# Gated cross-attention and expert layer on one core: records of 132 words, ScalarE forms the residual, another order of the half steps

## What is computed

```python
x = x + tanh(g_xattn[0]) * xattn(layernorm(x), ctx, ctx, W_qkv, b_qkv, W_out, b_out)
x = x + tanh(g_ffn[0]) * moe(layernorm(x), Wg, W1, b1, W2, b2)

# xattn, per batch and head (SCALE = 8 ** -0.5)
attn = softmax(q @ k.T * SCALE);  out = (attn @ v) merged over heads @ W_out + b_out
# moe (C = 4096 / 8 = 512)
gates = softmax(tokens @ Wg); idx = argmax(gates)        # first-come places, C per expert
hidden = relu(rows_of_expert @ W1[e] + b1[e]);  y = hidden @ W2[e] + b2[e]
out[token] = gate * y                                    # tokens beyond C get 0
```

## Time and profile before

| | us |
|---|---|
| median of 3 runs | 298.25 (296.54 to 298.52) |
| the profiled execution's own time | 298.6 |
| its span, from first to last instruction | 296.5 |
| PE busy, share of span | 244.5, 82% |
| DVE | 196.6, 66% |
| POOL | 182.3, 61% |
| ScalarE | 155.6, 52% |
| mean granted TensorE clock | 0.937 |
| DMA moved | 39.27 MB |

### The profile page before, as it was taken

How to read it: one execution, slowest core, us unless ns; L and a number is a source line. 1 busy time by engine, 2 the same in 40 slices (tenths; PEclk the granted TensorE clock), 3 DMA queues, 4 the chain that set the end, 5 groups by cost and what they waited for, 6 DMA issues and landing times.

```text
span 296.5 us, 8184 instructions
## 1 busy us (share of the span) xinstructions
PE 244.5 (82%) x2907; PEld 163.5 (55%) x2907; DVE 196.6 (66%) x663; ACT 155.6 (52%) x375; POOL 182.3 (61%) x246
## 2 busy tenths in 40 slices
PE   1748758788979989999899989995869999999950
PEld 1325525465755755765656666663324677777740
DVE  4676717647978999989897999965302545555440
ACT  5553727567778787787887756681202322222100
POOL 6625916911982998897897968448720056555781
PEclk9998959969999999999999999999595999999995
DMA  4652771990482652661733541138352256554310
GB/s 120 184 162 73 214 217 32 237 293 19 113 235 57 174 158 71 195 182 46 213 110 90 152 126 57 58 102 174 138 144 66 71 170 188 173 180 132 103 55 16
DMA packets 50920, 39.27 MB, mean 132 GB/s; under 512 B 9698, under 2 KB 47223, under 8 KB 50880
## 3 DMA queue, kind: packets, MB, share of 16 engines
q1 hardware_dynamic: 47168, 28.67, 35.9%
q0 software_dynamic: 3712, 10.07, 10.4%
HBM read 13.72 MB, written 12.65 MB: 89 GB/s over the span
## 4 chain that ended last, share of the span: by engine, by line
PE 39%; DVE 13%; DMA 13%; SPq 10%; issue 9%; ACT 8%; POOL 4%; POOLq 0%; ACTq 0%; DVEq 0%
PE X L634 9%; DMA qp<-mrow 8%; DVE negm L833 6%; SPq L347 6%; PE TS L618 5%; PE M L546 3%; ACT prob L703 3%; PE O L513 3%; PE TS L497 3%; PE O L618 3%; PE M L618 2%; PE S L482 2%; PE X L441 2%; SPq L358 2%; POOL rec_dram L1224 2%
## 5 line engine op out<-in xcount | busy, mean ns | idle before, releaser
L703 ACT ACTIVATE prob<-TS 128x512 f32<-128x512 f32 x128 | 72.0, 589 | 40.1 <-PE TS L497 39.2
L833 DVE TENSOR_REDUCE negm<-S 128x4 f32<-128x512 f32 x128 | 81.6, 679 | 8.5 <-PE S L482 7.9
L513 PE MATMUL O<-prob,vals 128*32 128x128 f32 x1024 | 42.1, 283 | 0.8 <-ACT oraw L712 0.8
L1313 POOL DMA_INDIRECT out_dram<-fin,tok x32 | 31.5, 986 | 14.2 <-issue 12.2
L1224 POOL DMA_INDIRECT rec_dram<-rec,slot x32 | 32.2, 1005 | 8.0 <-issue 5.5
L497 PE MATMUL TS<-qp,kp 64*128 64x128 bf16 x512 | 28.1, 221 | 9.7 <-DMA qp<-mrow 9.6
L482 PE MATMUL S<-kp,qp 62*128 62x128 bf16 x512 | 31.3, 222 | 2.3 <-DVE negm L833 2.0
L513 PEld LDWEIGHTS O<-prob,vals 128*32 128x32 f32 x1024 | 24.6, 110 | 13.9 <-ACT prob L703 7.0
L267 POOL TENSOR_TENSOR rest_k<-full_k,parts_k 128x512 f32<-128x512 f32 x7 | 8.0, 1149 | 39.3 <-ACT parts_k L674 39.3
L804 ACT ACTIVATE qp<-TS,b_act 128x512 f32<-128x512 f32 x16 | 11.0, 687 | 39.9 <-PE TS L618 39.9
L634 PE MATMUL X<-w2s,qp 128*128 128x128 f32 x240 | 28.2, 275 | 0.9 <-issue 0.9
(11 more groups left out here) (170 smaller groups left out, 486.8 us busy)
## 6 DMA issues: line engine op xcount, KB each, us to landing
kp<-parts_k SPq DMA_DIRECT2D x48, 128.0 KB, 2.5
qp<-parts_q SPq DMA_DIRECT2D x48, 128.0 KB, 4.1
rec_dram<-zeros POOLq DMA_DIRECT2D x8, 516.0 KB, 6.2
xr<-rec_dram SPq DMA_DIRECT2D x8, 260.0 KB, 3.9
x_sb<-in_x_dram SPq DMA_DIRECT2D x8, 256.0 KB, 3.6
c_sb<-in_ctx_dram SPq DMA_DIRECT2D x8, 256.0 KB, 3.5
out_dram<-rec SPq DMA_DIRECT2D x8, 256.0 KB, 3.3
w1s<-in_L_ffn_W_dram SPq DMA_DIRECT2D x8, 256.0 KB, 4.1
```

The costliest lines, as they stand in the source:

```text
L513: mm = nc.tensor.matmul(o_out[i * HV:(i + 1) * HV, u * L:(u + 1) * L], vals[G % 2][:, k, h, :], prob[n % 2][:, h * L:(h + 1) * L], start=( ...
L703: nc.scalar.activation(prob[n % 2][:, first:first + 4 * L], TS[:, a, :], ACT.Exp).then_inc(a_exp, 1)
L833: V.tensor_reduce(negm[n % 2][:, first:first + 4], S[:, a, :].rearrange("p (h k) -> p h k", k=L), AX.X, ALU.max, negate=True).then_inc(v_r ...
L1313: G_.indirect_dma_start(out_rows, bass.IndirectOffsetOnAxis(tok[p][:, t:t + 1], 0), fin[p][:, t, :], None, bounds_check=T - 1, oob_is_err= ...
```

## The change

- **Records** have 132 words: gate, token code, mean, deviation, then the 128 normalised values. Gate and code take the place of two of the logits in `rec`, the moments are aggregated right behind them, and the scatter sends from there. POOL gets one more multiplication per group, `deviation` (deviation = (var + eps) * (var + eps) ** -0.5). The zero writes and the scatters shrink with the record; `load_xr` goes, `load_xe` takes whole records into three buffers instead of two.
- **ScalarE** forms x1 again as normalised * deviation + mean (`rows_again`: four activations per expert), and DVE's `residual2` adds b2 * gate to that.
- **Heads** are numbered (h a) instead of (a h), so that one multiplication does the normalising instead of two.
- **Order of a step, PE**: scores u=0, shifted u=0, values u=0, maxima transpose, oT of c-5, group work, scores u=1, shifted u=1, values u=1, back, at, group work. Bank X0 now holds oT and at, M the maxima and back; xT and q move to X1.
- **Order of a step, ScalarE**: oraw of batch c-3 after the second exponentials, onT of c-5 after the first.
- **Order of a step, DVE**: top u=0, lower part, top u=1, normalise, residual, moments, group work.
- **SyncE** stores x1 of a group in step j = 1 instead of j = 0. POOL's scatters in a step wait for the lower part instead of the residual.

```diff
-REC = 2 * P + 2
+REC = P + 4
@@ x_tasks
-            bank0 = [("at", c - 5), second]
-            bank1 = [first, third]
-            bank2 = [("m", c - 1), ("back", c - 4), ("oT", c - 4)]
+            bank0 = [second] if c < 0 else [("oT", c - 5), ("at", c - 5)]
+            bank1 = [first, third] if c < 0 else [first, third, second]
+            bank2 = [("m", c - 1), ("back", c - 4)]
@@ SyncE, step
-                loads, stores = j == 0 and is_group(g + 2), j == 0 and is_group(g - 2)
+                loads, stores = j == 0 and is_group(g + 2), j == 1 and is_group(g - 2)
@@ SyncE, experts
-                sp.dma_start(xe[e % 2][:], rec_v[e][:, :, 0:D]).then_inc(xe_in[e % 2], 16)
-            def load_xr(e):
-                sp.dma_start(xr[e % 2][:], rec_v[e][:, :, D:REC]).then_inc(xr_in[e % 2], 16)
+                sp.dma_start(xe[e % 3][:], rec_v[e]).then_inc(xe_in[e % 3], 16)
...
@@ PE, step
                 if is_batch(c - 2):
                     shifted(c - 2, 0)
+                if is_batch(c - 3):
+                    values(c - 3, 0, 0)
+                    values(c - 3, 0, 1)
                 if is_batch(c - 1):
...
                     nc.tensor.transpose(m_out, negm[(c - 1) % 2][:], ident).then_inc(p_m, 1)
+                if is_batch(c - 5):
+                    bank_free(pe, "oT", c - 5)
+                    pe.wait_ge(v_on, c - 4)
+                    nc.tensor.transpose(oT_out, on[(c - 5) % 2][:], ident).then_inc(p_oT, 1)
...
+                if is_batch(c - 5):
+                    bank_free(pe, "at", c - 5)
+                    pe.wait_ge(a_oT, c - 4)
+                    nc.tensor.matmul(X[:, 0, 0:DE], onT[(c - 5) % 2][:], wout_g[:], start=True, stop=True).then_inc(p_at, 1)
@@ ScalarE, experts
+            def rows_again(e):
+                act.wait_ge(xe_in[e % 3], 16 * (e // 3) + 16)
+                if e >= 3:
+                    act.wait_ge(fin_out[e % 3], 64 * (e // 3))
+                for t in range(ET):
+                    mm = nc.scalar.activation(fin[e % 3][:, t, :], xe[e % 3][:, t, 4:], ACT.Identity,
+                                              bias=xe[e % 3][:, t, 2:3], scale=xe[e % 3][:, t, 3:4])
+                mm.then_inc(a_res, 1)
...
                 nc.scalar.activation(xeT[p][:], S[:, p, :], ACT.Copy).then_inc(a_eT, 1)
+                if e >= 1:
+                    rows_again(e - 1)
+                if e == E - 1:
+                    rows_again(e)
@@ DVE, normalise
-                for a in range(2):
-                    mm = V.tensor_tensor(on[n % 2][:, a * HALF:(a + 1) * HALF].rearrange("p (h d) -> p h d", d=HD),
...
+                V.tensor_tensor(on[n % 2][:].rearrange("p (h d) -> p h d", d=HD), o[:, :, 0:HD],
+                                rl[:].unsqueeze(2).broadcast_to([P, HEADS, HD]), ALU.mult).then_inc(v_on, 1)
@@ DVE, step
-                if is_batch(c - 5):
-                    residual(c - 5)
-                if is_batch(c - 4):
-                    normalise(c - 4, g - 2 if j == 0 and is_group(g - 2) else None)
...
                 if is_batch(c):
                     top(c, 1)
+                if is_batch(c - 4):
+                    normalise(c - 4)
+                if is_batch(c - 5):
+                    residual(c - 5)
@@ DVE, residual2
-                p = e % 2
...
+                dve.wait_ge(a_res, e + 1)
                 for t in range(ET):
                     mm = V.scalar_tensor_tensor(fin[p][:, t, :], b2_all[:, e, :], gate2[p][:, t:t + 1],
-                                                xr[p][:, t, 0:D], ALU.mult, ALU.add)
+                                                fin[p][:, t, :], ALU.mult, ALU.add)
@@ POOL
+            def deviation(G):
+                pool.wait_ge(g_rs2, G + 1)
+                G_.tensor_tensor(rec[G % 3][:, :, DEV], rs2[:, 0, :], rs2[:, 1, :], ALU.mult).then_inc(g_dev, 1)
...
-                G_.indirect_dma_start(rec_dram, bass.IndirectOffsetOnAxis(slot[p][:, k:k + 1], 0), rec[p][:, k, 0:REC], None,
+                G_.indirect_dma_start(rec_dram, bass.IndirectOffsetOnAxis(slot[p][:, k:k + 1], 0), rec[p][:, k, GATE:], None,
...
                 if j < 3 and is_group(g - 3) and g - 3 < NG - 2:
-                    pool.wait_ge(v_x1, min(c - 4, B))
+                    pool.wait_ge(v_m, min(c, B))
                     scatter(g - 3, j + 1)
```

More of the change, by code:

```diff
@@ L42, in flamingo_kernel @@
     DE = D + E
+    GATE, CODE, MEAN, DEV, NORMED = DE - 2, DE - 1, DE, DE + 1, DE + 2
     HEADS = 16
@@ L136, in flamingo_kernel @@
         st2 = sb("st2", [P, GB, 6])
-        mv2 = sb("mv2", [P, GB, 2])
         rs2 = sb("rs2", [P, 2, GB])
         nm2 = sb("nm2", [P, GB])
-        rec = [sb(f"rec{i}", [P, GB, D + DE]) for i in range(3)]
+        rec = [sb(f"rec{i}", [P, GB, NORMED + D]) for i in range(3)]
         lmax = sb("lmax", [P, GB])
@@ L161, in flamingo_kernel @@
         b1_dve = [sb(f"b1_dve{i}", [P, 1, FC]) for i in range(2)]
-        xe = [sb(f"xe{i}", [P, ET, D]) for i in range(2)]
-        xr = [sb(f"xr{i}", [P, ET, REC - D]) for i in range(2)]
+        xe = [sb(f"xe{i}", [P, ET, REC]) for i in range(3)]
         xeT = [sb(f"xeT{i}", [P, CAP]) for i in range(2)]
@@ L166, in flamingo_kernel @@
                for i in range(2)]
-        gate2 = [sb(f"gate2_{i}", [P, ET]) for i in range(2)]
-        tok = [sb(f"tok{i}", [P, ET], U32) for i in range(2)]
-        fin = [sb(f"fin{i}", [P, ET, D]) for i in range(2)]
+        gate2 = [sb(f"gate2_{i}", [P, ET]) for i in range(3)]
+        tok = [sb(f"tok{i}", [P, ET], U32) for i in range(3)]
+        fin = [sb(f"fin{i}", [P, ET, D]) for i in range(3)]
         s_cst, s_wqkv, s_bias, s_late = sem("s_cst"), sem("s_wqkv"), sem("s_bias"), sem("s_late")
@@ L412, in _ @@
                 load_w2(e)
-                sp.wait_ge(v_res, e - 1)
-                load_xr(e)
             for p in range(3):
                 sp.wait_ge(x1_out[p], 16 * len(range(p, NG, 3)))
-            for p in range(2):
-                sp.wait_ge(fin_out[p], 16 * ET * (E // 2))
+            for p in range(3):
+                sp.wait_ge(fin_out[p], 16 * ET * len(range(p, E, 3)))
         @block.tensor
@@ L532, in step @@
                     nc.tensor.transpose(m_out, negm[(c - 1) % 2][:], ident).then_inc(p_m, 1)
+                if is_batch(c - 5):
+                    bank_free(pe, "oT", c - 5)
+                    pe.wait_ge(v_on, c - 4)
+                    nc.tensor.transpose(oT_out, on[(c - 5) % 2][:], ident).then_inc(p_oT, 1)
                 for t in at_q[0]:
                     group_task(t[0], t[1])
-                if is_batch(c - 5):
-                    bank_free(pe, "at", c - 5)
-                    pe.wait_ge(a_oT, c - 4)
-                    nc.tensor.matmul(X[:, 0, 0:DE], onT[(c - 5) % 2][:], wout_g[:], start=True, stop=True).then_inc(p_at, 1)
+                if is_batch(c):
+                    scores(c, 1)
+                if is_batch(c - 2):
+                    shifted(c - 2, 1)
                 if is_batch(c - 3):
-                    values(c - 3, 0, 0)
-                    values(c - 3, 0, 1)
+                    values(c - 3, 1, 0)
+                    values(c - 3, 1, 1)
                 if is_batch(c - 4):
@@ L665, in proj @@
                 bias = bq_s[:, 0:1] if side == 0 else bqk[:, 1:2]
-                nc.scalar.activation(full[side][:], X[:, side, :], ACT.Identity, bias=bias,
+                nc.scalar.activation(full[side][:], X[:, 1, :] if side else q_bank(H), ACT.Identity, bias=bias,
                                      scale=(SCALE, 1.0)[side]).then_inc((a_qf, a_kf)[side], 1)
@@ L722, in step @@
                     exps(c - 2, 0, 1)
+                if is_batch(c - 5):
+                    n = c - 5
+                    act.wait_ge(p_oT, n + 1)
+                    if n >= 2:
+                        act.wait_ge(p_at, n - 1)
+                    nc.scalar.activation(onT[n % 2][:], oT_out, ACT.Copy).then_inc(a_oT, 1)
                 if j == (2 if g + 2 else 1) and is_group(g + 2):
@@ L1043, in step @@
                     top(c, 1)
+                if is_batch(c - 4):
+                    normalise(c - 4)
+                if is_batch(c - 5):
+                    residual(c - 5)
+                if j == 0 and is_group(g - 2) and g - 2 < NG - 1:
+                    moments2_ready(g - 2)
+                    moments2(g - 2)
+                if c == B + 4:
+                    route2(NG - 1)
+                    place2(NG - 1)
                 if j == 0 and is_group(g):
@@ L1154, in _ @@
             finish(E - 2, 0)
+            residual2(E - 1)
             finish(E - 2, 1)
             relus(E - 1)
-            residual2(E - 1)
             finish(E - 1, 0)
@@ L1168, in fence, with root @@
                 return G_.tensor_tensor(fence_p[:], pool_c[:, 0, 0:1], pool_c[:, 0, 0:1], ALU.add).then_inc(g_fence, 1)
-            def root(H, mv, rs, ready, e):
+            def root(H, var, rs, ready, e):
                 pool.wait_ge(ready, H + 1)
```

(5 more changed lines are left out.)

140 lines of the change are left out of this document (59 added, 81 removed).

## The result

The changed kernel takes 295.38 us (median of 20 runs, 293.02 to 302.56), the kernel before 298.38 beside it (20 runs). The ratio is 0.989, 95% interval 0.986 to 0.993: 1.1% faster, 3.2 us.

The account below looks back on a forecast made before the run. DMA traffic was taken to bound the first steps, with neither PE nor DVE free in steady attention. Early -5.5, steady -1.5 and bridge +1.9 sum to -5.1 from 298.6, so 293.5 us; 8 in 10 range 289 to 299.5.

Parts of the forecast that it names:

- likeliest case: Whole kernel: early steps and bridge as costed, steady steps within 3 us, 290.5 to 297 us; chance 0.55.
- steady term: Steady attention: -0.4 us per group over about 4 full groups, -1.5 us in all; bounds -6 and +6.
- early term: First steps: shorter zero writes free 6.0 us of path, later maxima DMAs cost 0.5; -5.5 us, bounds -2 and -8.
- bridge: Between attention and experts: the late row sum starts POOL about 1.5 us later; +1.9 us, bounds +0.4 and +3.
- sum by the fit: Whole kernel: by the fixed-cost DMA rule seven shorter zero writes give 4.1 us, and the sum would be 295.4.
- Scatters and loads: POOL's scatters and the load behind the last: width does not set issue time; 0, scatter bounds -0.3 to +0.2 us.
- ScalarE's residual: Experts: 1.9 us more ScalarE work per expert, covered by PE's outputs; 0, bounds 0 to +1 us.
- First expert: Experts: no gain was forecast, blocks were to keep the same length.
- A: First steps: zero writes do not hold the early landings, packs also fill the queues; early -1.5, 297.5 us; chance 0.2.
- B: Whole kernel: the order wins PE's idle back; early -7, steady -4.5, bridge +0.5, 287.6 us; chance 0.15.
- C: Steady attention: DVE loses its cover, maxima DMA lands late, 0.7 us in 3 steps of 7 groups; 306.9 us; chance 0.1.

Follow-up runs that it names:

- a_zero516: The changed kernel with each zero write as long as before (516 KB), records still 132 words: 303.58 us, 1.019 of the kernel before.
- a_store_j3: The changed kernel with the store of a group's rows in the fourth step of a group instead of the second: 296.13 us, 0.990 of before.
- a_maxima_first: The changed kernel with the maxima transpose ahead of the first half's values again on PE: 302.97 us, 0.978 of before.
- b_records2: The kernel b_records run again on another chip: 300.54 us, 0.967 of before.
- b_zero_gated: The kernel before with its full-size zero writes issued four at a time, POOL first waiting for the maxima rows of steps 3 and 7: 0.996 of before.
- r_dummies11: b_records with eleven dummy matmul pairs instead of eight ahead of the first expert: 300.89 us, 0.974 of before.
- r_best: b_records with ten dummy matmul pairs and its zero writes four at a time behind the lower parts of steps 3 and 7: 298.69 us, 0.969 of before.
- a_at_early: The changed kernel with, from the last scores on, PE's row sum ahead of the second values and DVE's residual ahead of normalise: 301.89 us, 0.970 of before.
- b_records: The kernel before with 132-word records, ScalarE's residual and three buffers, but its own order, banks, store and head numbering: 290.39 us, 0.976 of before.
- b_order: The kernel before with the new order, banks, head numbering and store in the second step, but records of 258 words: 313.89 us, 1.020 of before.

## Why the prediction was right, and where it was off

The direction and the likeliest case held, and 295.4 lies inside the case's own range of 290.5 to 297; 60% of the forecast gain came. It lies there in part by luck: the steady term was wrong by 3.7 us, and the early term, the bridge and an unforeseen gain in the first expert together made up 2.2 of them. Term by term:

**Early, -5.5.** Right in mechanism and size: -6.4 in the profiles at step 8, where a_zero516 stands 7.3 us behind after; in time it loses 1.0188 less 0.9893, 3.0% or 9 us (7.5 us against a_store_j3 on its own chip), so the extra bytes cost a little later on too. The size is read with care, as the same writes gave 3.2 us at step 8 in a_store_j3. My working scaled engine time with bytes. In 30:42 the share fell to 0.62 instead of 0.51 of what it was, in 53:67 to 0.30, since the writes there were over sooner. The Trainium skill (DMA: Bandwidth & Descriptors, the fixed-cost fit under "Anatomy of one DMA") gives, as an estimate, 4.1 us for the writes. The runs show 6.4 to 9 us. The fit is of one DMA; what transfers in full queues do to each other is seen here in 5.7 against 3.7 us of landing in 30:42, where the fit has 0.6 us between the two sizes. That the sum by the fit was 295.4, the time measured, is chance: both its early and its steady term were off.

**Steady, -1.5.** This is the step that failed, in its sign: +2.2 us from step 8 to 32. Two of the gains I listed came (`onT` 2.3 and the load's 1.3 us gone). The third did not: DVE's wait for the transposed output, 0.3 us a group to be saved, grew from 1.6 to 3.7 us in four. Of the losses I had DVE's idle before the reductions at 0.9 per group; it rose from 1.0 to 2.8 us in four, half of that. Missing was the other direction: PE's scores wait for DVE's reductions of the scores before, 4.2 us in 13 pieces. And I gave the later maxima rows 0.1 to 0.3 per group, where PE's wait for them rose by 0.7 (2.3 to 5.0 in four). I had followed that loop from DVE's side and counted the transpose's own shift; the table above shows the term that counts, PE's work between the transpose and the shifted scores, which the new order cuts from 4.6 to 3.57 us. Both lines stood in the trace of before: the transpose of the earlier trace rows and the wait of 0.71 on the next step's rows. New PE waits of 6.9 us less 3.6 gone are +3.3 in the window, of the size of the +2.2 to step 32. But the waits' own length is not what counts most: 1.3 of the 2.2 us go in the one step with the low clock behind the first wait, where two matmuls of 512 columns take 1.52 us (82.91) and 1.02 a group later at the same line. I had no term for that. Against the records alone on a like chip the order costs 3.8 to 4.4 us in steps 8 to 25. What stays open is the share of each piece in the time: no run took the wait for the maxima rows away whole, and those that moved it (a_store_j3, a_maxima_first) left waits between scores and reductions.

**Bridge, +1.9.** Right: +1.6 in the order's two kernels, 0.0 in the records alone, and POOL's idle grew by 1.75 us (4.74 to 6.49) where I had 1.5. Scatters and loads: 0 as said; a scatter takes 1003 ns for 132 words and 1005 for 258, and the last lands after 2.18 us instead of 2.30.

**ScalarE's residual, 0.** Right. Its group in after (line, engine, what, count, busy us, mean ns, idle before it):

```profile
L797 ACT ACTIVATE fin<-xe 128x128 f32<-128x128 f32 x32 | 13.0, 481 | 0.0
```

It is 13.0 us more of ScalarE, and from the third expert on an output block still takes PE 3.57 us, as in the earlier trace rows; nothing on PE waits for it.

**First expert, 0.** Unforeseen, -1.2 us. In both traces the clock is at 0.50 for a stretch that begins behind the last dummy: from 216.4 to 223.2 us in after, from 221.7 to 228.5 in before. After's turn starts later behind the dummies (4.8 us, 2.0 before), so only 4.6 us of this stretch fall on the expert's work, 6.8 before. These 2.2 us less at half the clock are worth 1.1 us, an estimate from the traces; the block is 6.7 us against 7.9. The other traces fit: 4.8 to 4.9 us where no low stretch touches the block (b_records2, b_zero_gated, r_dummies11, r_best), 6.5 and 6.6 with 3.4 us of one (a_at_early, b_records). What makes the clock fall in some and not in others I did not test.

**The rivals.** A fell with a_zero516. B fell: the order wins nothing back. C's mechanism is there, at a third of its size or less (2.8 us of DVE's waits in four groups, 1.0 of them before too, against 2.1 a group); but its condition, a later landing, was not what did it: the DMA took 1.98 to 2.53 us on after's chain in these steps.

## What to carry to other kernels

Where a tiny DMA is on the path and the queues are full, look for the bulk transfer that shares them and cut its bytes; moving it in time won at most 1% here, halving it 3%. Before an order is called neutral, measure for each round trip between engines how long the answer takes and how much work the asker has meanwhile (5.2 against 3.57 us here), and look at the waits in both directions, and at the granted clock behind each wait: one wait of 1.75 us cost 1.3 us with the low clock behind it, two of its size without it 0.1 and 0.9. A change with two halves deserves a run of each half: the good one (2.4%) carried a bad one (2.0% by itself, 1.4% by difference).

## What the runs showed of the hardware

- The same 4 KB transfer of maxima rows, where the chain runs through it, takes 1.98 to 2.53 us in after's steady steps, 3.5 and 3.9 in its early ones, 4.1 to 6.2 beside the long zero writes (before, a_zero516; 3.3 to 5.7 in b_order) and 8.45 behind a burst of four.
- Four writes of 516 KB issued within 3.2 us hold a 128 KB pack on the chain for 10.61 us.
- POOL's issue of a scatter takes 1003 ns with rows of 132 words and 1005 with 258.
- Of 15 waits of PE for the maxima rows of 1.5 to 2.6 us (steps 8 to 25, six kernels in the new order), 7 have a stretch at 0.50 of the clock on their heels. The five kernels that have one or two of them give back 2.2 to 5.0 us in these steps, the one without 0.4.
- In six of the eight profiles from the slower chips (all but a_at_early and a_maxima_first) one DVE instruction that computes places, on 128x4 elements and mostly 0.2 us long elsewhere, takes 1.7 to 2.1 us at 163 to 176 us, and the granted clock falls to 0.50 within 4 us. What holds it up no run shows.
- Chips differ more than the change is worth: the kernel before took 309.4 and 309.7 us on two of them, 298.8 on another (medians), at mean granted clocks of 0.922, 0.926 and 0.934.
